# State space stage of a two-layer decoder: both channel halves' products ahead of both scans, the second product in place in PSUM

## The reference

```python
dt = jax.nn.softplus(jnp.einsum('blr,rd->bld', dt_r, W_dt) + b_dt)
A = -jnp.exp(A_log)

def step(h, inp):
    dt_t, B_t, C_t, u_t = inp
    dA = jnp.exp(dt_t[:, :, None] * A)
    h = h * dA + dt_t[:, :, None] * B_t[:, None, :] * u_t[:, :, None]
    y = jnp.einsum('bdn,bn->bd', h, C_t)
    return (h, y)
```

## Time and profile before

| what | value |
|---|---|
| time, median of three runs | 1953.66 us (1953.19 to 1954.66) |
| span of the profiled execution | 1948.6 us |
| busy: PE, DVE | 1562.9 us (80%), 1491.3 us (77%) |
| busy: ACT, POOL | 953.5 us (49%), 920.7 us (47%) |
| the 32 x 8 steps, first product to last scan's end | 707.7 to 1284.5 us |
| granted TensorE clock, mean | 0.916 |

### The profile page before, as it was taken

How to read it: one execution, slowest core, us unless ns; L and a number is a source line. 1 busy time by engine, 2 the same in 40 slices (tenths; PEclk the granted TensorE clock), 3 DMA queues, 4 the chain that set the end, 5 groups by cost and what they waited for, 6 DMA issues and landing times. The chain is left out here.

```text
span 1948.6 us, 31799 instructions
## 1 busy us (share of the span) xinstructions
PE 1562.9 (80%) x10219; PEld 1017.4 (52%) x10219; DVE 1491.3 (77%) x2947; ACT 953.5 (49%) x1491; POOL 920.7 (47%) x938
## 2 busy tenths in 40 slices
PE   8889888989699978977878878769998811699991
PEld 4545547988476632322333333236776611588891
DVE  6899986887488779999989999967777678533335
ACT  3545543575544567657656666436566410011114
POOL 4455442444200147677676677654344100366653
PEclk8999998999899989999988999979999855799996
DMA  4000000000000000000000000020000040466654
GB/s 144 2 0 0 0 1 27 2 2 1 12 1 0 1 1 1 1 1 0 0 1 0 0 0 1 1 78 11 5 9 5 3 145 0 159 209 206 212 171 135
DMA packets 49075, 75.34 MB, mean 39 GB/s; under 512 B 8861, under 2 KB 34821, under 8 KB 48437
## 3 DMA queue, kind: packets, MB, share of 16 engines
q1 hardware_dynamic: 43541, 64.12, 10.5%
q0 software_dynamic: 4544, 9.32, 1.6%
q10 hardware_dynamic: 864, 0.33, 0.1%
HBM read 62.26 MB, written 11.48 MB: 38 GB/s over the span
## 5 line engine op out<-in xcount | busy, mean ns | idle before, releaser
L1506 POOL TENSOR_TENSOR m_hC<-m_h,m_Cs 128x512 f32<-128x512 f32 x256 | 328.2, 1287 | 169.2 <-DVE m_h L1680 122.6
L1788 PE MATMUL PS<-m_hC,identf 128*128 128x512 f32 x512 | 296.5, 662 | 100.9 <-POOL m_hC L1506 99.9
L1680 DVE TENSOR_TENSOR_SCAN m_h<-m_dA,PS 128x512 f32<-128x512 f32 x256 | 312.4, 1220 | 11.2
L1788 PEld LDWEIGHTS PS<-m_hC,identf 128*128 128x128 f32 x512 | 93.0, 203 | 236.4 <-POOL m_hC L1506 208.9
L1675 DVE TENSOR_TENSOR PS<-PS,m_DU 128x512 f32<-128x512 f32 x256 | 178.4, 697 | 19.9 <-issue 3.8
L1616 ACT ACTIVATE m_dA<-m_DT,m_A 128x508 f32<-128x508 f32 x256 | 174.3, 714 | 31.3 <-DVE m_DT L1664 31.1
L1996 ACT ACTIVATE e_Sg<-PS 128x512 f32<-128x512 f32 x71 | 42.4, 597 | 223.0 <-PE PS L2238 178.8
L2238 PE MATMUL PS<-e_xT,e_WT 128*128 128x128 f32 x1136 | 143.8, 281 | 4.9 <-DVE e_xT L2146 3.4
L1608 ACT COPY m_Cs<-PS 128x512 f32<-128x512 f32 x128 | 73.7, 576 | 143.7 <-PE PS L1766 143.5
L2238 PEld LDWEIGHTS PS<-e_xT,e_WT 128*128 128x128 f32 x1136 | 135.4, 195 | 9.3 <-DVE e_xT L2146 7.1
L1935 POOL DMA_INDIRECT e_XG<-token_rows,e_ids x71 | 68.8, 969 | 138.9 <-DVE e_ids L2140 117.6
(11 more groups left out here) (411 smaller groups left out, 3801.6 us busy)
## 6 DMA issues: line engine op xcount, KB each, us to landing
e_WT<-in_w_wgu SPq DMA_DIRECT2D x71, 512.0 KB
token_rows<-X SPq DMA_DIRECT2D x2, 2048.0 KB
e_Y<-expert_rows SPq DMA_DIRECT2D x16, 256.0 KB, 4.0
k_BD<-in_w_bcr SPq DMA_DIRECT2D x1, 2464.0 KB, 9.5
e_w_wd<-in_w_wd SPq DMA_DIRECT2D x1, 2048.0 KB, 7.9
out_dram<-X SPq DMA_DIRECT2D x8, 256.0 KB, 2.4
X<-in_x SPq DMA_DIRECT2D x1, 1792.0 KB, 8.7
x_Cs<-in_ctx SPq DMA_DIRECT2D x8, 154.0 KB
```

The costliest lines, as they stand in the source:

```text
L1506: nc.gpsimd.tensor_tensor(hC[:, i % ND, :], hst[:, i % ND, :], Cs[:, n % ND, :], ALU.mult).then_inc(s["hC"], 1)
L1680: nc.vector.tensor_tensor_scan(hst[:, i % ND, :], dA[:, i % NA].rearrange("p b l -> p (b l)"), bank(4), 0.0, ALU.mult, ALU.add).then_inc(s ...
L1788: nc.tensor.matmul(bank(5 + ch), c.identf[:, :], hC[:, i % ND, :], start=False, stop=(n == NS - 1)).then_inc(s["yacc"], 1)
```

## The change

In DVE's step, even steps now make the products of both halves: that of half 0 into bank 4 as before, that of half 1 in place over the spread B, in bank 1 or 2. Odd steps do both scans. The second product waits for the first (which reads the same B); scan 0 has no wait for a product any more, scan 1 waits for product 1; the first product waits for scan 0 of the pair before (the last reader of bank 4) in place of the scan just ahead. `spread_b` waits for both scans of the state that had its bank, since a scan is now its last reader.

```diff
             def step(g, par, i, left):
-                n, ch = i // CH, i % CH
-                if i < CH:
-                    dve.wait_ge(s["du"], g * CH + i + 1)
-                if ch == 0:
+                n = i // CH
+                held = (4, 1 + n % 2)
+                if i % CH == 0:
                     dve.wait_ge(s["B"], g * NS + n + 1)
-                if not first(g, i, 1):
-                    dve.wait_ge(s["h"], g * NI + i)
-                nc.vector.tensor_tensor(bank(4), bank(1 + n % 2), DU[:, par, ch, :], ALU.mult).then_inc(s["dBu"], 1)
-                dve.wait_ge(s["dBu"], g * NI + i + 1)
-                dve.wait_ge(s["dA"], g * NI + i + 1)
-                if not first(g, i, ND):
-                    dve.wait_ge(s["hC"], g * NI + i - ND + 1)
-                nc.vector.tensor_tensor_scan(hst[:, i % ND, :], dA[:, i % NA].rearrange("p b l -> p (b l)"), bank(4), 0.0, ALU.mult, ALU.add).then_inc(s["h"], 1)
+                    if not first(g, i, CH):
+                        dve.wait_ge(s["h"], g * NI + i - 1)
+                    for ch in range(CH):
+                        if n == 0:
+                            dve.wait_ge(s["du"], g * CH + ch + 1)
+                        if ch == 1:
+                            dve.wait_ge(s["dBu"], g * NI + i + 1)
+                        nc.vector.tensor_tensor(bank(held[ch]), bank(1 + n % 2), DU[:, par, ch, :], ALU.mult).then_inc(s["dBu"], 1)
+                    return
+                for ch in range(CH):
+                    u = n * CH + ch
+                    if ch == 1:
+                        dve.wait_ge(s["dBu"], g * NI + u + 1)
+                    dve.wait_ge(s["dA"], g * NI + u + 1)
+                    if not first(g, u, ND):
+                        dve.wait_ge(s["hC"], g * NI + u - ND + 1)
+                    nc.vector.tensor_tensor_scan(hst[:, u % ND, :], dA[:, u % NA].rearrange("p b l -> p (b l)"), bank(held[ch]), 0.0, ALU.mult, ALU.add).then_inc(s["h"], 1)
...
                 if not first(g, n, 2):
-                    pe.wait_ge(s["dBu"], g * NI + CH * (n - 1))
+                    pe.wait_ge(s["h"], g * NI + CH * (n - 1))
```

## The result

| kernel | median of five runs | ratio to before |
|---|---|---|
| before | 1954.66 us (1953.19 to 1958.92) | 1 |
| after | 1933.02 us (1931.14 to 1938.41) | 0.9896, 95% interval 0.9881 to 0.9911 |

The change makes the kernel 20.3 us faster, by the ratio.

What follows compares the result with a forecast made beforehand. VectorE was taken to bound only the last group (-5.75 us); groups 0 to 6 were held by a chain through PE, ACT and POOL, summing to 0. So 1953.7 - 5.8 = 1947.9 us, range 1936 to 1956.

Steps and rivals of the forecast that it cites:

- (d): POOL's corrections to next gate: POOL busy 18.1 us without a gap, VectorE's gain goes into its gate wait, nothing won.
- (b): x0 to B's spread for steps 18 and 19: PE nearly gapless, 15.83 us; VectorE waits about 2.2 us at product 18.
- The pair, 0.42 us less: Two products and two scans on VectorE: fewer waits take a plain pair from 4.05 to 3.63 us.
- R2: Rival: VectorE drains between instructions anyway, so fewer waits gain nothing; 1953.7 us, chance 0.08.
- The product in place, 0: Second product reading and writing one PSUM bank: no extra cost taken, bounds 0 to 0.42 us.
- R4: Rival: the product in place takes longer; at 1.12 us the last group wins nothing, 1955 us, chance 0.04.
- (a): Gate to the input projection's first matmul (x0) in a middle group: does not move, 18.9 us for 18.98.
- (c): Last projections to POOL's corrections: VectorE's later scan 18 enters through hC 18, 0.2 us longer.
- Groups 2 and 4, -0.45 each: Groups behind the loop's branch, where VectorE stands 1.88 us: scan 8's end decides, about 0.45 us won in (a).
- (e): Last group, VectorE the bound: 13 plain pairs 5.46, statistics pair 0.29, last pair 0.23, against 0.23 lost; -5.75 us.
- R1's half-way case: Rival: the chain follows VectorE for one part more, 1.5 us in each of seven groups; 1937 us, chance 0.12.
- R3: Rival: later first scans slow the middle groups' chain, 1.5 us in each of seven groups; 1958.4 us, chance 0.14.

Runs made afterwards that it cites:

- the filling: Spreads of B and C done three times at steps 5 to 8 and 24 to 31 (also "clock held up"): before 0.9952, after 0.9865.
- the filled before: Kernel before, with the spreads of B and C done three times at steps 5 to 8 and 24 to 31: 1945.35 us, ratio 0.9952.
- the first trace of after: Profile of the changed kernel's first run, 1933.02 us; the second is the same kernel run again unchanged, 1934.66 us.
- the moved kernel: Changed kernel, output statistics and norm behind step 7, residuals behind 19 and 21; spreads tripled at steps 5 to 8: 1945.75 us; with the filling 1934.33.
- the filled after: Changed kernel, with the spreads of B and C done three times at steps 5 to 8 and 24 to 31: 1929.95 us, again 1930.78.

## Why the prediction was wrong, by its own steps

What failed is the sum for groups 0 to 6, forecast as 0 and measured as -9.7 us. The largest part is step (d), which took two accumulations at TensorE's lower level as a fixed length of the chain. Beside it, two waits for VectorE were taken as fixed: the gap in (b) and the stop at the loop's branch.

- **The pair, 0.42 us less: right in kind, too small.** Measured 4.05 - 3.56 = 0.49. The plain scans and products are each a little shorter when they overlap (1201 and 690 ns), and by starts two scans take 2.24 for 2.28, product 1 to scan 0 0.61 for 0.62, products 0.71 apart for 0.74. Waits are what it comes from: with all of them back it is 4.10, with one back 3.76. R2 falls with this. By the section on the DRAIN in the Trainium skill's page "VectorE: DVE Perf Modes" the waits would have been free; these runs show 0.5 us a pair for three of them. The same section adds that a next operation that is not held starts earlier, which the prediction left out, and with that the 0.08 us of overlap agree.
- **The product in place, 0: right.** 690 ns in after. R4 falls.
- **(a) Gate to x0, 18.9 for 18.98: right on the engines that it looked at, wrong in the sum.** 20.11 to 20.53 was measured, since steps 7 and 8's accumulations now fall in a stretch at 0.56 of the clock. With the clock held up it is 18.89.
- **(b) Waits at product 18 and at `rest`: right; the length of PE's row, 15.83 us: too fixed.** VectorE waits 1.93 and 0.93 us, where 2.2 and a second were forecast (1.2 + 5 x 0.42 less 0.94 is 2.4, slightly more than it says). Idle time before products for B is 19.0 us in all. But the gap in "PE has no gap but one of 0.14 us" was a wait for VectorE's scan through hC, and with the slower start behind it it held PE up by 0.4 us. The change takes it away.
- **(c) x0 to the corrections, +0.2: wrong.** 33.16 to 33.21 in all six groups of after, as in the groups of before without a slow stretch there (33.18, 33.17). Scan 18 through hC 18 does not hold up the chain. The 33.58 of group 3, from which I worked, had in it the 0.4 us of (b), which the change takes away, with the filling too (34.36 against 33.96).
- **(d) Corrections to gate, unchanged: this is the step that failed by most.** "POOL is busy without a gap for 18.1 us", it said, "PE adds two accumulations, and VectorE waits 1.80 us for the gate", and it took these two accumulations as given. Their rows were 2.08 and 1.92 us, where two matmuls of the kind take 1.12 at full clock. The prediction had costed such matmuls itself, at 0.43 us a start, in (b). I priced the chain's work with TensorE's clock as it stood in one trace, as if the change couldn't move it. It moved the slow stretches away from five gates, 1.3 to 1.9 us each and 7.7 in all, and from inside groups 2 and 4. With the filling this piece is 18.36 to 18.40 us in groups 1 to 6 of both kernels. Nor did VectorE's gain go into a wait at the gate: its 11.6 us there in all fell to 5.6, 2.7 of it at the last gate, and it waits for B, for the cast and for POOL's logarithm (L1664) instead.
- **Groups 2 and 4, -0.45 each: mis-sized.** -3.54 and -5.66. Filled, the difference is -2.9 and -2.6. 1.3 of each is a stretch at 0.50 of the clock at x0, left in before; 0.4 is that of (b); the rest, 1.2 and 0.9, lies ahead of x0. There the prediction took VectorE's 1.88 us at the branch as fixed, and they became 1.26 to 1.56.
- **(e) The last group, -5.75: mis-sized, in two terms.** To the end of the last scan 62.88 became 55.85, -7.03 for -5.98: the 0.07 us more a pair. From there to the gate 3.50 became 2.67, -0.83 where +0.23 was forecast, and that is the clock again. Before, its last accumulation:

```profile
1285.87 2.08 PE L1788 MATMUL PS<-m_hC,identf 128*128 128x512 f32 x2 [0.85 <-POOL m_hC L1506]
```

and in the filled before, with VectorE's rows the same:

```profile
1279.66 1.13 PE L1792 MATMUL PS<-m_hC,identf 128*128 128x512 f32 x2 [0.86 <-POOL m_hC L1506]
```

  That 0.95 us is the whole difference of group 7 between the two (66.38 and 65.43).
- **The rivals.** R1's half-way case came nearest in number (1937), and its mechanism, a chain that follows VectorE for one part more, is there: with the clock held up the odd groups gain 0.5 us and groups 2 and 4 1.3 to 1.6, some 4 us over groups 1 to 6. It is not the 1.5 us in each of seven groups that gave the 1937, so the nearness of the number is in part luck. R3's mechanism is real when the waits are kept (2.0 us a group), and the fewer waits outweigh it. What was missing is a rival that asks what the change does to a clock that depends on how busy the engine is. It is not on the list.

Account of the 20.3 us: about 7 for VectorE in the last group; about 1 for the clock in its tail; some 10 in groups 0 to 6 by the first trace of after, 6 by the second. Of the 10, about 4 are VectorE's part by the filled kernels (three groups at 0.5, two at 1.3 to 1.6, less 0.3 that group 6 loses), and about 6 are left for stretches at 1.2 GHz; this split is an estimate from single traces. Filling alone took 9.8 us from before (1955.10 to 1945.35) but 3.9 from after by medians (1934.66 to 1930.78). The rest, 2.7 us behind the last gate, is scatter.

**Still open.** Why a stretch falls ahead of x0 in after and ahead of the gate in before was not foreseen by any of the expectations and isn't explained by the runs: PE was busy 1.4 to 3.0 of 4 us ahead of those looked at, and as thinly once with no fall behind it. Nor is it known why VectorE stands 0.5 us less at the loop's branch without the wait between the scans and 0.9 more in the moved kernel, why after has a trace with more stretches, nor whether group 0 gains anything: its period is 73.11 and 75.27 us in the two traces of the filled after.

## What to carry to other kernels

Ahead of pricing a chain, list TensorE's rows on it and compare each with the same matmul elsewhere in the trace: a row that takes twice as long is a stretch at half the clock (check the granted clock there), and an unrelated change of a few tenths of a microsecond can move it on or off the chain. Two such experiments decide at little cost: the kernel before with TensorE kept busy at the suspected places, and the change with one small delay put back. Then look at how much of the gain is left at the same mean clock: here two thirds of it in the middle groups were, in part real waits and in part a stretch that the filling missed. A gap of 0.14 us in a row that looks full is a wait too; ask who ended it. A wait for the instruction just ahead on VectorE costs 0.15 to 0.2 us where VectorE is the bound, even if what it waits for is always there in time; interleaving two independent chains on one engine removes it.

## What the runs showed of the hardware

- An instruction of VectorE that doesn't wait for the one ahead starts 0.08 us before that ends; one that does starts 0.03 to 0.11 behind its end. One such wait between two scans costs 0.20 us a pair, three of four 0.49.
- Reading and writing the same PSUM bank in one product costs nothing: 690 ns for 697.
- TensorE's granted clock fell to half for a few microseconds, behind windows in which PE was busy 1.39 and 1.70 of 4 us at full clock, but also behind 3.04 of 4 us; behind 1.64 of 3.90 it once did not fall. Two matmuls that took 1.12 us took 1.8 to 2.1 in it. Two or four more small matmuls in the gaps, 0.22 us each, kept it at 1.00 at the two places filled. It can make a kernel with more work faster (0.9952), and one wait a pair, which costs 3 us in the last group and 3 to 4 in the others with the clock held up, made the changed kernel 16 us slower without (0.9979 for 0.9896).
- At the loop's branch VectorE stood 1.86 to 2.13 us in the kernels where the last scan ahead of it waits for the instruction just ahead, 1.26 to 1.56 where it doesn't, and 2.79 to 2.93 with the output statistics right ahead of the branch.
- An instruction of VectorE with both inputs in SBUF takes longer beside POOL. In the steps of groups 0 to 6 softplus's last instruction (L1664) took 1032 ns before and 1753 after, where its inputs come from POOL's corrections just then:

```profile
L1664 DVE SCALAR_TENSOR_TENSOR m_DT<-m_DT,m_L 128x512 f32<-128x512 f32 x14 | 14.4, 1032 | 0.4 <-POOL m_L L1491 0.4
```
```profile
L1664 DVE SCALAR_TENSOR_TENSOR m_DT<-m_DT,m_L 128x512 f32<-128x512 f32 x14 | 24.5, 1753 | 7.8 <-POOL m_L L1491 7.8
```

  The first row is of before, the second of after (x14, total and mean, then idle time ahead). The Trainium skill's page "SBUF — State Buffer", section "Who interferes with whom", says that a VectorE instruction with two SBUF inputs contends with a GpSimd instruction that reads SBUF, and the one that comes second stands until the first has finished; the trace agrees: before, the second of a group started with 0.20 us left of POOL's instruction and took 0.75 us, and after, with 1.22 us left, 1.77. The 10.1 us of it in all cost nothing that shows: VectorE reaches the gate with 0.24 us to wait.
